# A counting sort on one core: windows of 24 lanes with runs of 16 records instead of 25 lanes with runs of 8

## The reference

```python
def _spmm(row, col, vals, x):
    msg = vals[:, None] * x[col]
    return jax.ops.segment_sum(msg, row, num_segments=N)      # N = 12500, E = 400000

def _layer(x_prev, row, col, vals, W_a, b_a, W_b, b_b):
    h = _spmm(row, col, vals, x_prev)
    z = (h + x_prev) @ W_a.T + b_a + h * x_prev @ W_b.T + b_b
    return jnp.where(z >= 0, z, NEG_SLOPE * z)

x = emb[x_ids]
x1 = _layer(x, row, col, vals, W1_1, b1_1, W1_2, b1_2)
x2 = _layer(x1, ...)
x3 = _layer(x2, ...)
return jnp.concatenate((x, x1, x2, x3), axis=1)
```

## Time and profile before

| | before |
|---|---|
| median of 3 runs | 10850.23 us (10849.24 to 10851.59) |
| the profiled execution's own time | 10898.8 us |
| its span in the profile | 10896.9 us |
| PE, DVE busy | 9894.6 us (91%), 8103.6 us (74%) |
| ACT, POOL busy | 4422.0 us (41%), 5560.2 us (51%) |
| windows of pass 0, first rank to last order | 333.3 to 1989.1 us |
| windows of pass 1 | 2403.1 to 4114.9 us |
| the three layers | about 4417 us to the end |

### The profile page before, as it was taken

The page is one execution under the profiler, slowest core; times in us unless marked ns, Lnnn a source line. Parts: engine busy times, 40 slices in busy tenths (PEclk is TensorE's granted clock), DMA queues, the critical chain, the costliest instruction groups (busy, mean ns, idle before and its releaser), DMA issues.

```text
span 10896.9 us, 237080 instructions
## 1 busy us (share of the span) xinstructions
PE 9894.6 (91%) x72468; PEld 8991.3 (83%) x72469; DVE 8103.6 (74%) x11525; ACT 4422.0 (41%) x13847; POOL 5560.2 (51%) x3315
## 2 busy tenths in 40 slices
PE   6899999669889884899999999999999999999999
PEld 4677777547777773799899998999999999999999
DVE  7877777668777774677777777777777777777777
ACT  0466666216666660455311125553111256531112
POOL 7477777207777771000488860004888600058885
PEclk8666666766666665899999999999999999999999
DMA  2111111101111119899988879999888699988886
GB/s 75 26 4 4 4 4 4 14 6 4 4 4 4 4 4 24 261 338 331 298 287 287 286 245 287 340 333 299 285 286 286 232 310 341 330 295 285 287 286 215
DMA packets 1186670, 1966.67 MB, mean 180 GB/s; under 512 B 455636, under 2 KB 506904, under 8 KB 1185976
## 3 DMA queue, kind: packets, MB, share of 16 engines
q0 software_dynamic: 467360, 1031.62, 32.7%
q1 hardware_dynamic: 719256, 934.47, 30.0%
HBM read 1212.56 MB, written 752.96 MB: 180 GB/s over the span
## 4 chain that ended last, share of the span: by engine, by line
PE 40%; DMA 16%; ACT 3%; issue 2%; DVE 1%; SPq 0%; POOL 0%; ACTq 0%; DVEq 0%; POOLq 0%
PE ps L910 33%; DMA messages<-work 16%; PE ps L901 5%; ACT work L668 3%; PE ps L881 1%; PE ps L938 1%; PE ps L918 1%; PE ps L939 1%; PE ps L928 0%; SPq L586 0%; DVE work L1162 0%; DMA work<-messages,work 0%; DVE work L1245 0%; DMA hT<-sorted_edges 0%; POOL sorted_edges L484 0%
## 5 line engine op out<-in xcount | busy, mean ns | idle before, releaser
L509 POOL DMA_INDIRECT work<-messages,work x1920 | 2931.9, 1527 | 3732.6 <-issue 3730.0
L910 PE MATMUL ps<-work 128*128 128x125 f32 x30720 | 3549.2, 278 | 37.5 <-DVE work L1273 37.5
L910 PEld LDWEIGHTS ps<-work 128*128 128x128 f32 x30720 | 3505.9, 192 | 80.8 <-DVE work L1273 38.1
L484 POOL DMA_INDIRECT sorted_edges<-stage,run_idx x1270 | 2422.6, 1908 | 1461.2 <-DMA sorted_edges<-stage,run_idx 537.5
L901 PE MATMUL ps<-xb,work 125*128 x21504 | 2473.6, 277 | 186.6 <-DVE work L1245 106.4
L901 PEld LDWEIGHTS ps<-xb,work 125*128 125x128 f32 x21504 | 2429.5, 193 | 230.6 <-issue 228.0
L794 PEld LDWEIGHTS ps<-hT 128*128 128x128 f32 x12700 | 2175.5, 271 | 421.1 <-issue 396.9
L794 PE MATMUL ps<-hT 128*128 128x80 f32 x12700 | 2180.7, 356 | 314.4 <-ACT hT L627 230.2
L1273 DVE TENSOR_TENSOR work<-work,iota_p 128x1000 f32<-128x1000 f32 x1920 | 2291.9, 1194 | 34.4 <-ACT work L686 34.4
L668 ACT ACTIVATE work<-ps,work 128x128 f32<-128x128 f32 x5376 | 1507.0, 372 | 1325.2 <-DMA messages<-work 806.4
L686 ACT ACTIVATE work<-work 128x8 f32<-128x8 f32 x1920 | 577.7, 301 | 2883.4 <-DMA work<-messages,work 2883.4
(11 more groups left out here) (200 smaller groups left out, 4110.2 us busy)
## 6 DMA issues: line engine op xcount, KB each, us to landing
messages<-work SPq DMA_DIRECT2D x2688, 256.0 KB, 6.4
work<-slot_cols SPq DMA_DIRECT2D x672, 256.0 KB, 6.2
work<-messages,work POOLq DMA_INDIRECT x1920, 5.9
sorted_edges<-stage,run_idx POOLq DMA_INDIRECT x1270, 3.2
out_x<-xb SPq DMA_DIRECT2D x150, 125.0 KB
work<-lane_places SPq DMA_DIRECT2D x508, 5.5 KB, 3.3
out_x<-xb SPq DMA_DIRECT2D x4, 1562.5 KB
sorted_edges<-hT SPq DMA_DIRECT2D x4, 906.0 KB
```

Source lines behind the costliest of these rows:

```text
L484: pool.indirect_dma_start(out=sorted_edges[p], out_offset=bass.IndirectOffsetOnAxis(ap=run_idx[:, q, k:k + 1], axis=0), in_=stage[:, q, k ...
L509: pool.indirect_dma_start(out=ck[:, n, :, :].rearrange("p h x -> p (h x)"), out_offset=None, in_=octs, in_offset=bass.IndirectOffsetOnAxis ...
L910: last = t.matmul(part[n], ck[:, n, j // CH, j % CH * D:(j % CH + 1) * D], sel[:, n % SELB, j, :], start=j == 0, stop=j == CHB - 1)
```

## The change

A window has 24 lanes instead of 25 and a run 16 records instead of 8, so the scattered rows have 128 bytes instead of 64; there are 3 runs for each partition instead of 5, and 48 slots instead of 40. The lanes no longer divide by 24, so both passes are padded: 3,144 and 3,240 lanes, 131 and 135 windows. The padding of the raw edges is filled by three memsets. ACT builds 18 of the 24 lanes of `to_part` instead of 19 of 25, and DVE the same 6. `in_slot` has one buffer instead of two, since two of the larger size don't fit.

```diff
+LANES = 24
+FILLED = E // P
+COLS = -(-FILLED // LANES) * LANES
+TILES1 = -(-(FILLED + NB) // LANES) * LANES
...
-LANES = 25
...
-RUN = 8
-RUNS = 5
+RUN = 16
+RUNS = 3
 SLOTS = RUN * RUNS
...
-ACTL = 19
+ACTL = 18
...
+        beyond = [work[:, k * COLS + FILLED:(k + 1) * COLS] for k in range(3)]
...
-        in_slot = [hT[:, IS0 + q * SLOTW:IS0 + (q + 1) * SLOTW].rearrange("p (l c) -> p l c", c=SLOTS) for q in range(2)]
+        in_slot = hT[:, IS0:IS0 + SLOTW].rearrange("p (l c) -> p l c", c=SLOTS)
...
+            for k in range(3):
+                link(v.memset(beyond[k], 0.0 if k else 1.0))
...
                 dve.wait_ge(slot_link, n + 1)
-                v.tensor_tensor(in_slot[q], slot[:, :, None].to_broadcast([P, LANES, SLOTS]),
+                if not first:
+                    dve.wait_ge(moved_ready, n)
+                v.tensor_tensor(in_slot, slot[:, :, None].to_broadcast([P, LANES, SLOTS]),
                                 iota_s[:, None, :].to_broadcast([P, LANES, SLOTS]), ALU.is_equal).then_inc(in_slot_ready, 1)
...
                 for f, field in enumerate((packed[p], value[p])):
-                    last = v.tensor_tensor(moved[q][:, :, f, :], in_slot[q],
+                    last = v.tensor_tensor(moved[q][:, :, f, :], in_slot,
```

More of the change, by code:

```diff
@@ L38 @@
 PAIR = 2 * BLK
-COLS = E // P
-TILES1 = E // P + NB
+LANES = 24
+FILLED = E // P
+COLS = -(-FILLED // LANES) * LANES
+TILES1 = -(-(FILLED + NB) // LANES) * LANES
 TABW = -(-TILES1 // P)
 LT = TABW * P
-LANES = 25
 WINDOWS = [COLS // LANES, TILES1 // LANES]
@@ L204, in graph_layers @@
         IS0 = MV0 + 4 * SLOTW
-        in_slot = [hT[:, IS0 + q * SLOTW:IS0 + (q + 1) * SLOTW].rearrange("p (l c) -> p l c", c=SLOTS) for q in range(2)]
-        assert IS0 + 2 * SLOTW <= ABODIES * ZC
+        in_slot = hT[:, IS0:IS0 + SLOTW].rearrange("p (l c) -> p l c", c=SLOTS)
+        assert IS0 + SLOTW <= ABODIES * ZC
         zeros = hT[:, 12544 - 2000:12544 - 2000 + ZW]
@@ L517, in _ @@
                 dst = (raw_row, raw_col, raw_val)[k]
-                sp.dma_start(dst, src.rearrange("(p c) -> p c", p=P)).then_inc(edges_in, DMA)
+                sp.dma_start(dst[:, 0:FILLED], src.rearrange("(p c) -> p c", p=P)).then_inc(edges_in, DMA)
             sp.dma_start(ids_c[:, :], ids.rearrange("(c r) -> c r", r=BLK)).then_inc(ids_in, DMA)
```

## The result

The changed kernel takes 10223.6 us in the median (10220.25 to 10226.38, four runs) against 10850.9 us, a ratio of 0.9422 with a 95% interval of 0.9405 to 0.9438: 5.8% faster. The prediction said 10650 us, with a range of 10530 to 10790, so the direction was right and the gain three times as large as forecast: 627 us where 201 were expected.

The account below looks back on a forecast made before the run. POOL's pace of 13.15 us was taken to bound the sort windows before the change. Windows -122, tables -47, tails -34 and small costs +2 made -201 us off 10850, rounded to 10650 us; range 10530 to 10790.

Parts of the forecast that it names:

- POOL's pace as the bound of before: Sort windows: POOL's five indirect DMAs plus the landing take 13.1 us, so the mean of 13.26 is POOL's pace.
- The formula for the mix: Sort windows: PE's low-clock work divided by clock shares and busy shares, times 1.024, gave 12.2 us a window, 122 us gained.
- the clock stays high: Sort windows: PE's waits too short for the clock to fall, DVE sets 10.7 us, total 10250 us; chance 0.06.
- a granted clock above 0.72: Sort windows: a mean granted clock below 0.60 or above 0.72 would show the prediction wrong.
- Its first sign of being right: Sort windows: POOL's first scatter of a window waits for ACT's `stage` instead of a landing.
- PE's pitch at 96 columns: Order bursts on PE: matmuls of 96 columns cost no more than 80; burst 10.30 us low, 5.41 high.
- DVE's chain: Sort windows on DVE: 10.45 us without a wait plus 0.25 gives 10.7 us for a window.
- POOL's issues: Scatters on POOL: no growth with bytes, three issues of 1.91 us each, 8.6 us a window with the landing.
- Tables: Table loops: 0.22 us off each step, less 12 more steps, a gain of 47 us (24 to 95).
- Tails: End of each sort pass: one scatter left instead of two, 8.1 to 9 us, 34 us gained over both.
- The new wait on `moved_ready`: DVE in the sort windows: waiting on its own `moved_ready` costs nothing; a semaphore's 0.1 us if cover were gone.
- the terms outside the windows: Table loops, pass tails and small costs (histograms, scans, memsets): -47, -34 and +2 us, together -79 us.

Follow-up runs that it names:

- the run with three scatters: The kernel before with only the first 3 of the 5 scatters of each window issued, all other work the same: 10135.0 us, ratio 0.9304.
- four scatters: The kernel before with only the first 4 of the 5 scatters of each window issued: 10135.4 us, ratio 0.9319.

## Why the prediction was right and wrong

**POOL's pace as the bound of before: right.** 13.1 us by its own cycle, 13.26 measured; taking scatters away is enough to free it (10.38 us), giving POOL two DMAs back is enough to bind again (11.97), and changing the geometry alone leaves the pace (13.11).

**The formula for the mix: wrong, and this is the step that failed.** It took the shares of the two clock levels (0.296 and 0.704) from the kernel before and kept them, "which is a choice". From that followed 12.2 us a window, bound in effect by PE's work at 1.2 GHz. In the changed kernel the low share is a third, and the windows go at DVE's pace. The low share belonged to the kernel that it was read from. The formula came within 2.4% of the kernel before (12.87 us against 13.17) only because it describes PE's time however PE is bound: work divided by clock and busy share, both read from the same rows, and it says nothing of what ends the waits. With the changed kernel's own low share (0.34) and busy share of PE (0.87, from its stretches above) it gives 14.38 / (0.87 x (0.34 + 0.66 x 1.90)) x 1.024 = 10.6 us, what was measured, as an identity must. With the low share alone put right and the idle shares as forecast it gives 9.8, so the idle shares were guessed too small as well. That PE's work at the low clock sets no pace is shown by the run with three scatters, where the same work on PE went through in 10.38 us a window.

**The rival "the clock stays high"** had the right number: 10250 us from DVE's 10.7 us a window. Its mechanism was half right. The clock does still fall, for 3.4 or 6.8 us at a time, but this costs nothing that can be measured: PE would need the forecast 14.38 us only in a window wholly at 1.2 GHz, and with stretches of 6.8 us at most there is none; a window at 2.4 GHz takes 7.55. The argument against it, that PE still idles 3 us, was true (2.83 and 2.89 us) and didn't matter. I gave it 0.06, where the plain rule of the slowest engine's chain would have led straight to it. The prediction names a granted clock above 0.72 as a sign that it is wrong, and that sign came (0.83). Its first sign of being right mostly did not: of the waits of POOL ahead of a first scatter between 700 and 1500 us, 52 were ended by a landing and 20 by ACT's `stage`.

**Terms.** PE's pitch at 96 columns: a burst at the high clock took 5.49 us for 48 records, against 5.70 for 50, so no cost of columns, as taken. No burst of 96 columns was wholly at the low clock, so the 10.30 us there were not measured. The rule of the Trainium skill (TensorE: Matmul & The Clock Gate, Part 1), that back-to-back matmuls start their number of columns divided by the clock apart, doesn't hold between these fp32 matmuls of 80 and 96 columns, each with its own weights. DVE's chain: forecast 10.7, measured 10.51; the growth of 0.25 us was right, and the 10.45 us it was added to held a longer small instruction (0.38 us instead of 0.18) in that one window. In the kernel with three scatters the chain of 25 lanes takes 10.24 us (the first scatters of its windows, below, are that far apart), and 10.24 + 0.25 is 10.49. POOL's issues: forecast 1.91 us each, measured 2.47; the bytes are not the reason, as the same 3 issues of 64 bytes take 3.75, 1.67 and 1.92 us (2.40 on average over all windows) where DVE runs without a stop. Tables: 118.5 us became 62.0 + 33.6 = 95.6 in pass 0, and both passes gave 51 us against 47 forecast. Tails: in pass 0 the last order burst ended at 1712.7 us and the load went out at 1720.91, 8.2 us where 8.1 to 9 were forecast; in pass 1 it is 3503.8 and 3512.88 us, 9.1. The new wait on `moved_ready` shows nowhere. The three layers were unchanged apart from the difference between executions. So the terms outside the windows held, -84 us where -79 were forecast.

**Open.** Why half of the low stretches last 20 us or more at a pace of 13.2 us, and none over 6.8 us in the changed kernel at 10.5, is not settled. The place of the wait doesn't explain it: with two more DMAs PE waited ahead of its order bursts again, up to 4.3 us, and the clock was still 0.79 and 0.85, with low stretches of 3.4 to 10.2 us.

## What to carry to other kernels

When engines form a ring of buffers (each works on buffers that another must first fill or free), compare each engine's own cycle, with its fixed waits, and let the longest set the pace. An average clock of TensorE that is read from a kernel whose PE waits for others is an outcome and can't be carried over to a kernel with another bound. The cheap test is to change the suspected pace alone (leave some of its DMAs out) and, separately, to raise the clock with matmuls that nothing reads; these must stand where PE idles, or they eat what the clock gives back. Once the pace is freed, work that can be moved off the next engine (here lanes of `to_part` from DVE to ACT) was worth its full length in each window. And an engine that looks full may only be held: POOL's issues filled the period because they stood behind DVE.

## What the runs showed of the hardware

A scatter's issue on POOL takes 1.54 us when it meets nothing (all six issues behind 1706 us at the end of pass 0 in the changed kernel take 1.54 to 1.56) and up to 4.1 us beside DVE. The timeline of POOL in the kernel with three of five scatters shows the first issue stretched in both windows, which are 10.24 us apart:

```profile
903.73 3.75 POOL L485 DMA_INDIRECT sorted_edges<-stage,run_idx  x1 [2.29 <-DMA sorted_edges<-stage,run_idx]
907.79 1.67 POOL L485 DMA_INDIRECT sorted_edges<-stage,run_idx  x1 [0.31 <-issue]
909.76 1.92 POOL L485 DMA_INDIRECT sorted_edges<-stage,run_idx  x1 [0.30 <-issue]
913.97 3.76 POOL L485 DMA_INDIRECT sorted_edges<-stage,run_idx  x1 [2.29 <-DMA sorted_edges<-stage,run_idx]
```

Most of this is one rule that the traces show without an exception. An issue that begins while DVE's bf16 one-hot (`one_hot`) is running ends 1.40 to 1.49 us behind the end of the one-hot, whenever in it the issue began. That holds for all 622 such issues between 700 and 1500 us in nine of the ten kernels (four scatters has none; issues that began in the last 0.1 us of a one-hot are left out). So the issue is held until the one-hot is through. In the changed kernel this ties POOL to DVE: the one-hot ends at 714.25, POOL has done its three issues and the landing by 722.52, 8.27 us later, and there it enters the issue that must wait for the one-hot of 722.10 to end, at 724.76. POOL has some 2.2 us to spare in a window, although it looks full.

The Trainium skill, GPSIMD Engine Reference, section 1 (Specifications), has POOL share its interfaces to SBUF with VectorE, with contention when a DVE instruction reads two inputs from SBUF; the one-hot is such an instruction (L1070 from 711.59 us on for 2.66 us in the changed kernel, the stretched issue from 712.19 on), and the trace agrees, though no run took it away. But two inputs alone don't give the size: the issue of 715.97 us ran beside L1098 and L1102, which read two inputs as well, and took 1.83 us. Why the one-hot holds an issue for its whole length and these don't is not shown. The effect of this on a sum of issues is large: four scatters fit into 10.28 us, and five take 13.2. Rows of 128 bytes took little longer to land than rows of 64: POOL waited 2.28 and 2.35 us for them, against 2.22 in the earlier trace rows and 2.29 for the rows of 64 bytes above.
